# A seventh buffer in the ring of states, and projection weights that come through the ring of streamed weights

## The reference, cut to what matters

```python
xn = layernorm(x) * (1 + scale) + shift             # scale, shift, gate from c
x_in, z = split(xn @ in_proj_w.T)                   # 1024 channels each
u = silu(causal_conv4(x_in) + conv_b)
dt_r, B, C = split(u @ x_proj_w.T, [64, 80])        # the projection: 64 + 16 + 16 rows
dt = softplus(dt_r @ dt_proj_w.T + dt_proj_b)
for t in range(2048):                               # per channel and per state n of 16
    h = h * exp(dt[t] * A) + dt[t] * u[t] * B[t]
    y[t] = sum_n(h * C[t])
x1 = x + gate * (((y + u * D) * silu(z)) @ out_proj_w.T)
```

## Time and profile before

| | |
|---|---|
| median of 3 runs | 2237.83 us (2236.24 to 2241.0) |
| the profiled execution | 2238.82 us, of which 2237.0 us from its first to its last instruction |
| PE busy | 2040.1 us (91%) |
| DVE busy | 1985.6 us (89%) |
| POOL busy | 1744.8 us (78%) |
| ACT busy | 1674.5 us (75%) |
| DMA, mean | 99 GB/s |

### The profile page before, as it was taken

How to read it: one execution, slowest core, us unless ns; L and a number is a source line. 1 busy time by engine, 2 the same in 40 slices (tenths; PEclk the granted TensorE clock), 3 DMA queues, 4 the chain that set the end, 5 groups by cost and what they waited for, 6 DMA issues and landing times.

```text
span 2237.0 us, 31435 instructions
## 1 busy us (share of the span) xinstructions
PE 2040.1 (91%) x10240; PEld 1320.8 (59%) x10240; DVE 1985.6 (89%) x2245; ACT 1674.5 (75%) x3186; POOL 1744.8 (78%) x1139
## 2 busy tenths in 40 slices
PE   8889989988998999899989988999868899999999
PEld 3355555545555554555555555545545688888878
DVE  4899999989999999999999999999999766666666
ACT  3688797878887888888887889887677455466655
POOL 0599999999999999999999999999999422232225
PEclk9899999999999999999999999999988999999999
DMA  6623342352234143434342351334001211111113
GB/s 219 240 83 95 97 165 67 85 171 85 76 98 176 57 104 81 175 99 99 107 149 66 86 191 56 84 93 179 29 29 55 99 34 36 37 53 62 41 57 132
DMA packets 122592, 220.73 MB, mean 99 GB/s; under 512 B 24317, under 2 KB 39933, under 8 KB 122430
## 3 DMA queue, kind: packets, MB, share of 16 engines
q1 hardware_dynamic: 122430, 218.74, 31.5%
HBM read 171.91 MB, written 17.30 MB: 85 GB/s over the span
## 4 chain that ended last, share of the span: by engine, by line
PE 44%; issue 15%; DVE 14%; POOL 11%; ACT 11%; DMA 3%; SPq 1%; DVEq 0%; POOLq 0%; ACTq 0%
PE ps L516 15%; DVE arena L1094 9%; PE ps L297 9%; POOL arena L1529 8%; PE ps L368 6%; DVE arena L1082 5%; PE ps L358 3%; ACT arena L654 3%; ACT ps L654 3%; PE ps L344 2%; ACT L654 2%; POOL arena L1493 2%; PE ps L324 2%; ACT L754 1%; PE ps L510 1%
## 5 line engine op out<-in xcount | busy, mean ns | idle before, releaser
L1529 POOL TENSOR_TENSOR arena<-arena 128x1024 f32<-128x1024 f32 x512 | 1199.8, 2362 | 97.3 <-ACT arena L654 93.8
L1094 DVE TENSOR_TENSOR_SCAN arena<-ps,arena 128x512 f32<-128x512 f32 x1024 | 1189.3, 1202 | 13.0 <-ACT ps L654 12.0
L654 ACT ACTIVATE ps<-arena 128x512 f32<-128x512 f32 x1087 | 713.2, 677 | 207.7 <-DVE arena L1082 105.6
L368 PEld LDWEIGHTS ps<-keep,arena 128*128 128x128 f32 x4096 | 475.0, 144 | 311.0 <-POOL arena L1529 170.7
L368 PE MATMUL ps<-keep,arena 128*128 128x128 f32 x4096 | 540.8, 281 | 117.9 <-POOL arena L1529 100.0
L1082 DVE TENSOR_TENSOR arena<-ps,arena 128x1024 f32<-128x1024 f32 x398 | 476.7, 1198 | 22.4 <-PE ps L368 18.2
L297 PE MATMUL ps<-arena 128*128 128x512 f32 x1024 | 469.2, 600 | 12.4 <-issue 11.5
L297 PEld LDWEIGHTS ps<-arena 128*128 128x128 f32 x1024 | 188.0, 192 | 229.4 <-issue 228.9
L1493 POOL TENSOR_TENSOR arena<-arena 128x1024 f32<-128x1024 f32 x114 | 269.3, 2362 | 17.2 <-PE ps L368 17.1
L358 PE MATMUL ps<-arena 128*128 128x512 f32 x512 | 238.1, 601 | 1.7 <-DVE arena L1115 1.7
L654 ACT ACTIVATE arena<-ps 128x512 f32<-128x512 f32 (+2 forms) x330 | 168.4, 526 | 77.4 <-PE ps L297 58.2
(11 more groups left out here) (153 smaller groups left out, 2683.4 us busy)
## 6 DMA issues: line engine op xcount, KB each, us to landing
arena<-in_inT SPq DMA_DIRECT2D x184, 256.0 KB, 2.8
arena<-scr_bc SPq DMA_DIRECT2D x80, 512.0 KB, 10.0
arena<-arena SPq DMA_DIRECT2D x224, 128.5 KB, 2.4
arena<-scr_bc SPq DMA_DIRECT2D x48, 511.0 KB, 9.5
arena<-in_x SPq DMA_DIRECT2D x17, 512.0 KB, 3.7
scr_x<-arena SPq DMA_DIRECT2D x32, 256.0 KB, 2.0
arena_b<-scr_x SPq DMA_DIRECT2D x16, 512.0 KB, 3.6
arena_c<-scr_x SPq DMA_DIRECT2D x32, 256.0 KB, 2.9
```

Source lines behind the costliest of these rows:

```text
L368: last = e.matmul(YP[:, 128 * q:128 * q + 128], hb[G % R][:, i, 128 * q:128 * q + 128], ident, start=(g == 0 and i == 0 and q == 0), stop= ...
L654: return e.activation(o_, i_, f, **kw)
L1094: e.tensor_tensor_scan(H, DA[s % 4], H, 0.0, MUL, ADD).then_inc(v_sc)
L1529: e.tensor_tensor(H, H, Ct[:, GN * g:GN * g + GN, :], MUL).then_inc(g_w)
```

## The change

R goes from 6 to 7: the ring has a seventh buffer, `hb_last`, in room that `wxp` leaves (the arena's other parts are shuffled so that everything from `Ct` on keeps its address). Every wait of `expand` becomes `p_y >= G - 6` instead of `G - 5`. The projection of the first chunk takes its weights from `wx0`, a view of the still unused `Ct`. For the other seven chunks the weights come through `win`, in two halves (uses 24 and 25 in `WSEQ`), so that 14 loads of 256 KB are added; each half's buffer is handed back by `p_w`, and `proj_evac` waits for `p_w` instead of `p_xp`.

```diff
-    NCH, NU, NG, GN, R = 8, 64, 8, 2, 6
+    NCH, NU, NG, GN, R = 8, 64, 8, 2, 7
...
+        hb_last = sb(GN, T)
         Ct = sb(16, T)
+        wx0 = Ct[:, 0:2, :].rearrange("p a b -> p (a b)").rearrange("p (k n) -> p k n", k=8)
...
+        hb = [hb_all[:, i, :, :] for i in range(R - 1)] + [hb_last]
...
+                if (j, pr) in PROJ and c + 1 < NCH:
+                    WSEQ += [(c + 1, 24 + h) for h in (0, 1) if PROJ[j, pr][0] < 4 * h + 4 <= PROJ[j, pr][1]]
...
-                    last = e.matmul(P, wxp[:, q, :], u[c % 2][:, q, :], start=(q == 0), stop=(q == 7))
-                if hi == 8:
+                    no = p_no(c, q // 4)
+                    if q % 4 == 0:
+                        e.wait_ge(d_win[no % 4], 16 * (no // 4 + 1))
+                    last = e.matmul(P, win[no % 4][:, q % 4, :], u[c % 2][:, q, :], start=(q == 0), stop=(q == 7))
+                    if q % 4 == 3:
+                        last.then_inc(p_w)
...
-                e.wait_ge(p_xp, c + 1)
+                e.wait_ge(*((p_w, p_no(c, 1) + 1) if c else (p_xp, 1)))
...
-                e.dma_start(win[no % 4], A["inT"][i]).then_inc(d_win[no % 4], 16)
+                src = A["inT"][i] if i < 24 else A["xpT"][512 * (i - 24):512 * (i - 24) + 512, :].rearrange("(k p) n -> p k n", p=128)
+                e.dma_start(win[no % 4], src).then_inc(d_win[no % 4], 16)
...
+                if (j, pr) in PROJ and more:
+                    used += sum(1 for h in (0, 1) if PROJ[j, pr][0] < 4 * h + 4 <= PROJ[j, pr][1])
```

More of the change, by code:

```diff
@@ L63, in program @@
         xt, xe = sb(2, 514), sb(516)
-        wxp, xdbl[0], gbc[1], wdt = sb(8, 128), sb(T), sb(512), sb(1024)
-        xnT[1], win = sb(4, T), [sb(4, 128) for _ in range(4)]
+        win = [sb(4, 128) for _ in range(2)]
+        xdbl[0], gbc[1], wdt = sb(T), sb(512), sb(1024)
+        xnT[1], win = sb(4, T), win + [sb(4, 128) for _ in range(2)]
+        hb_last = sb(GN, T)
         Ct = sb(16, T)
+        wx0 = Ct[:, 0:2, :].rearrange("p a b -> p (a b)").rearrange("p (k n) -> p k n", k=8)
         dt, xr, spt, xdbl[1], xs, sz = [sb(T) for _ in range(2)], [sb(512) for _ in range(2)], sb(T), sb(T), sb(2, 512), sb(3, T)
@@ L69, in program @@
         gbc[0] = xdbl[1]
-        hb_all = sb(R, GN, T)
-        hb = [hb_all[:, i, :, :] for i in range(R)]
+        hb_all = sb(R - 1, GN, T)
+        hb = [hb_all[:, i, :, :] for i in range(R - 1)] + [hb_last]
         scP = hb_all[:, 2, 0, 0:256].rearrange("p (a b) -> p a b", a=8)
@@ L227, in program @@
         c_no = lambda c, i: w_no[c, 16 + i]
+        p_no = lambda c, h: w_no[c, 24 + h]
         kept = lambda U: U // 8 % 4 < 3
@@ L343, in proj @@
                         e.wait_ge(a_su, su_of(c) - (q == 0))
-                    last = e.matmul(P, wxp[:, q, :], u[c % 2][:, q, :], start=(q == 0), stop=(q == 7))
-                if hi == 8:
+                    if c == 0:
+                        last = e.matmul(P, wx0[:, q, :], u[0][:, q, :], start=(q == 0), stop=(q == 7))
+                        continue
+                    no = p_no(c, q // 4)
[4 more added lines that the diff above has]
+                        last.then_inc(p_w)
+                if c == 0:
                     last.then_inc(p_xp)
@@ L441, in _ @@
                         conv_mm(c + 1, CMM[j, pr])
+                    if more and (j, pr) in PROJ:
+                        proj(c + 1, *PROJ[j, pr])
                     if (j, pr) in ZMM and U + ZMM[j, pr][0] < NU:
                         z_mm(U + ZMM[j, pr][0], *ZMM[j, pr][1:])
-                    if more and (j, pr) in PROJ:
-                        proj(c + 1, *PROJ[j, pr])
                     if c > 0 and (j, pr) in OUTM:
@@ L1656, in _ @@
             stream_w(4)
-            e.dma_start(wxp, A["xpT"].rearrange("(k p) n -> p k n", p=128)).then_inc(d_ws, 16)
+            e.dma_start(wx0, A["xpT"].rearrange("(k p) n -> p k n", p=128)).then_inc(d_ws, 16)
             e.dma_start(wdt[0:65, :], A["dtT"]).then_inc(d_ws, 16)
```

## The result

The changed kernel takes 2243.34 us (median of 20 runs, 2236.92 to 2248.43), the kernel before 2237.09 us beside it (20 runs). The ratio is 1.0023, with a 95% interval of 1.0015 to 1.0031: slower by some 5 us. The forecast was 2240.4, its range reached to 2246. The result lies in the range; the sign of the sum was right (+2.6 us), its size half of what came.

What follows compares the result with a forecast made beforehand. DVE was taken to set the scan stage's pace, with a chain of ACT, DMAs, PE and POOL setting each chunk's end; -0.4 us (ring) and +3.0 us (streaming) on the median of 2237.83 gave 2240.4 us, range 2234 to 2246.

Steps and rivals of the forecast that it cites:

- the sum: Whole kernel: -0.4 us for the seventh buffer and +3.0 us for streaming the projection's weights make +2.6 us.
- The ring: Seventh buffer in the scan stage: gains only 0.4 us, between 0 and 18.2; the other waits move to ACT and POOL.
- the 18.2 us: 23 waits of DVE's `expand` for PE's `nsum`, nearly all in units 6 and 7, at which the seventh buffer aims.
- the first rival: Scan stage: the seventh buffer pays and the 18.2 us go, giving 2222.6 us, or 2234.8 for a third; chance 0.13.
- the chain: Chunk end, 53.9 us in chunk 1: ACT, shift, PE, store, `B0` and POOL set the next chunk's start, not ring buffers.
- The load ahead of the store: Chunk end: a 256 KB load 0.7 us ahead delays the store 0.5 us at six boundaries, +3.0 us (0 to 7.2).
- a late shift: Eighth shift: it lands late and delays PE at every boundary, up to 2245.8 us; chance 0.22, shared with a later store.
- The small pieces: First-half projection load, 512-byte pieces ahead of the eighth shift: flight of 3.7 us, delaying the shift by any excess over 3.5.
- One of the signs that would have shown the forecast wrong: Eighth convolution starting later after its shift than before; the other sign was DVE's scan-stage idle time falling over 5 us.
- The store's bound of 1.2 us: Chunk end: the store, 1.6 us alone, takes all of a shift's 2.8 us; 2244.6 us, within the slower case's 0.22.
- the late weights: Projection at step (6, 15): its weights come late and PE waits; chance under 0.01, counted in the slower case.
- the cover of 17 us: Projection's first-half weights: loaded at 451.78, used near 469, 17 us later, so their waits cost PE nothing.

Runs made afterwards that it cites:

- e1: The changed kernel with seven buffers but no weights streamed for the projection, whose matmuls take the identity: 2235.97 us, 0.9990 of the kernel before.
- e4: The kernel before with the eighth convolution at step (6, 11) instead of (6, 9) on PE: 2225.80 us, 0.9937 of the kernel before.
- e11: The kernel before with the weight load of step (7, 4) waiting for the projection, so just ahead of the store: 2241.14 us, 1.0009 of the kernel before.
- e3: The changed kernel with the weight load held back behind the store of B and C: 2237.91 us, 0.9999 of the kernel before.
- e12: The changed kernel with eight filler identity matmuls while PE waits for the eighth shift, and the load behind the store: 2231.30 us, 0.9964 of the kernel before.
- e9: The changed kernel with eight filler identity matmuls on PE while it waits for the eighth shift: 2237.16 us, 0.9999 of the kernel before.
- e10: The kernel before with eight filler identity matmuls on PE while it waits for the eighth shift: 2230.96 us, 0.9970 of the kernel before.
- e7: The changed kernel measured and profiled once more, without edit: 2244.46 us, 1.0030 of the kernel before.
- e2: The changed kernel with six buffers instead of seven, streaming kept: 2241.87 us, 1.0012 of the kernel before.
- e8: The kernel before measured and profiled once more, without edit: 2239.34 us, ratio 1.0005.
- e5: The changed kernel with the eighth convolution at step (6, 11) instead of (6, 9): 2224.98 us, 0.9941 of the kernel before.

## Why the prediction was right, and where it was short

**The ring (-0.4 us): right.** That the 18.2 us would change their name was the step most open to doubt, and the first rival hung on it. The waits show it in every detail named: for `nsum` 1.9 us (below 5 was said), more of scans for ACT, at step (7, 2) in all seven chunks (1.05 to 3.49 us) and at (7, 9) in six (1.16 us), `expand` held by `first_column` at six boundaries. e1 bounds the whole at -2.2 us (0 to -4.5 us), and e4 says why: the chain ahead set the end, and an edit to the chain moved it. The Trainium skill (Perfetto Trace Analysis, section Identifying Performance Opportunities) says that consistent bubbles can mean too few buffers. By that reading the 18.2 us would have gone; the 0 to 4.5 us of e1 are against it here.

**The load ahead of the store (+3.0 us): right place, sign and mechanism; the size is not settled.** The load was issued within 0.01 us of ACT's start, where 0.1 was said. The store landed after 2.03 to 2.34 us (2.0 to 2.2 was said), and 0.5 us a boundary came out as 3.2 us at the six gated ones. At one of them (chunk 4 to 5) the store of the kernel before had taken 2.2 us already, with no load near it, which the 1.6 of the earlier trace rows, a median, hides; at the other five it rose by 0.4 to 0.6 us. So the term was well read, and e11 (+2.0 us) agrees with it. But e3 gives 5.4 us and e12 against e9 7.8, and only the last of these leaves the 3.0 outside its range. Whether the load costs more in the changed kernel than in the one before is not shown.

**What the sum lacked: PE's clock.** The prediction took PE's stretch of 17.6 us as given. The row that it read had the half clock in it: 0.90 for the stretch, and 2.80 us for a convolution that takes 1.94 in four other chunks of that profile and 3.4 and 3.6 in two. It didn't ask whether the other chunks had the same, or what would happen if one more fell. In the profiles it made +3.1 us between the landing and the projection, and +1.7 us in units 0 to 5: more than the 2.5 us by which the sum fell short. Two profiles of each kernel can't say how much of it belongs to the change, and with the clock evened out at the convolution the two kernels still lay 6.5 us apart (e9, e10). That the time is in the range all the same is in part luck: the range reached to 2246 for the sake of a late shift, which did not come.

**The small pieces: read rightly, and no rival.** The flight was priced at 3.7 us as an estimate, and the load of the first half took just that in chunk 1; the median of the fourteen is 3.0 (2.6 to 3.8). The changed kernel's rows, of 451.82 and of all:

```profile
arena<-in_xpT SPq DMA_DIRECT2D x1, 256.0 KB, 3.7
...
arena<-in_xpT SPq DMA_DIRECT2D x14, 256.0 KB, 3.0
```

It was to matter where it flew longer than 3.5 us, by the excess. The shift was issued at 455.44, ACT's copy being 0.19 us later than before; with 3.62 us between them the excess was nothing to speak of. Where there was an excess, it did not do what the rival said: at chunk 0's end in e7 the load flew for 4.69 us with the shift 3.34 us behind it, and the convolution started 4.21 us after the shift, as in the other chunks. There the load still in flight did not hold up the shift. One of the signs that would have shown the forecast wrong did come, in small: the eighth convolution of chunk 1 started 5.36 us after its shift's first DMA, where it was 4.96. From the start of unit 6 to the landing it is 19.96 to 20.19 us in chunk 1 of all eight profiles with seven buffers, and 19.17 to 19.69 in the six with six. e1 has it too, without a single small piece, and e2 has not, with all of them. So it belongs to the ring, not to this rival, at 0.3 us or more for one chunk; how is open.

**The store's bound of 1.2 us, the late weights:** neither came in the changed kernel's profiles, where the store's worst were 2.34 us and, in e7, 2.55. PE's matmuls of the projection start without a gap that the change made, so that the cover of 17 us was enough, as said.

**The sum.** Predicted +2.6 us; measured +5.1 by the ratio (3.4 to 6.9). The forecast is outside that interval, so the sum is too small by an amount clear of noise, though the time is within the range. By pieces of the profiles it is +3.6 (store) -1.0 (given back behind it) +3.1 +1.7 (clock) +0.4 (shift), 7.8 us over seven chunks. The last chunk and what lies outside the stage give 2.3 back, which is their scatter, so that the spans differ by 5.5 in the mean. At the seventh boundary, which has no `B0`, the store's delay is given back in full, as said: from the store to the new chunk 11.9 us instead of 12.4. Chunk lengths rose by 1.1 us in the mean, not by 0.5.

**Open.** Why the clock is at its half at these places more often; why e1 and e2 don't add up to the change; what holds e9 and e10 apart. The load's place may have to do with the clock or not. With the load ahead of the store the convolution at (6, 9) ran at the half clock in 18 of 28 chunks (changed, e7, e2, e11), with the load behind it in 14 of 28 (before, e8, e1, e3). Unit 1 was over 27.3 us in 14 of 36 chunks with it ahead (those four, e5 and e9) and in 11 of 48 with it behind (the other eight). These counts are too near to each other and too few to call it shown, and two profiles of one kernel differ in one or two such places. So of what the load's place is worth, some 3 us are shown by its own rows; if it is worth more, that the rest is the clock was not forced one way and the other.

## What to carry to other kernels

A wait that repeats is worth what the next wait behind it leaves. Follow one place in order of time to the chain that sets its end before pricing a deeper ring, and try to move the chain first (here two steps in a table gave 14 us, and the buffer 0 to 4.5). When an edit shifts the count in an in-order DMA queue, look for the one load that now leaves just ahead of a transfer on the chain: here, moving it behind the transfer was enough to undo the change's loss. Price PE's stretch at both clocks that the trace shows, and count in how many chunks each stands, before calling it fixed.

## What the runs showed of the hardware

After the same idle wait PE went on at either clock: 2.50 us of idling and then 1.00, 2.53 us and then 0.50, in the same chunk of two kernels; within one profile, too, chunks with the same queue differ (2.53 us before the full clock in chunk 2 of the kernel before, 2.18 us before the half clock in its chunk 3). The half clock at this convolution cost 1.4 to 1.65 us each time, 2.8 in chunk 1 of the changed kernel. The total of its stretches in the scan stage was the same, 102.4 us, in four profiles of two kernels in which such convolutions were 3, 4, 5 and 5: the place decides, not the total. Eight small matmuls of the identity in the wait kept it at 1.00 in all fourteen places of e9 and e10, and gave 5 to 7 us back for nothing but otherwise idle time.

In the changed kernel's profile a 64 KB store 0.7 us behind a 256 KB load lands after 2.0 to 2.3 us instead of 1.6 (2.55 and 2.89 once each in e7 and e9). 256 KB in pieces of 512 bytes fly for 3.0 us in the median (2.6 to 3.8; 4.7 once in e7), in pieces of 2 KB for 2.8. 2048 single numbers take 8.0 us in the median.
